# One attention group's division and pair transpose moved out of the run of row maxima, behind the first two maxima of a later group

## What is computed

```python
xn = _layernorm(x)
q = (xn @ wq).reshape(4, 512, 32, 16); k = (xn @ wk).reshape(4, 512, 8, 16); v = (xn @ wv).reshape(4, 512, 8, 16)
# rope on q and k; each of the 8 key heads serves 4 query heads
scores = einsum('bqhd,bkhd->bhqk', q, k) / 4 + causal_mask
attn = softmax(scores)                       # exp(score - row maximum), then a division by the row sum
s = einsum('bhqk,bkhd->bqhd', attn, v).reshape(4, 512, 512) @ wo
g = silu(top-2-of-8 experts: mean of relu(xn @ W_e + b_e))
x = x + s * g
# second layer: layer norm, a long convolution (S4 kernel made from its spectrum), gated by a linear layer
```

## Time and profile before

| | us |
|---|---|
| median of 3 runs | 697.06 (695.39 to 698.77) |
| the profiled execution's own time | 695.48 |
| its span, first to last instruction | 693.3 |
| PE busy | 638.2 (92%) |
| DVE busy | 553.4 (80%) |
| POOL busy | 351.1 (51%) |
| ACT busy | 289.0 (42%) |
| mean granted TensorE clock | 0.97 of full |

### The profile page before, as it was taken

The page is one execution under the profiler, slowest core; times in us unless marked ns, Lnnn a source line. Parts: engine busy times, 40 slices in busy tenths (PEclk is TensorE's granted clock), DMA queues, the critical chain, the costliest instruction groups (busy, mean ns, idle before and its releaser), DMA issues.

```text
span 693.3 us, 12356 instructions
## 1 busy us (share of the span) xinstructions
PE 638.2 (92%) x3560; PEld 344.0 (50%) x3560; DVE 553.4 (80%) x1789; ACT 289.0 (42%) x535; POOL 351.1 (51%) x497
## 2 busy tenths in 40 slices
PE   8999997888989999989999898999998999999997
PEld 4888774433333334333443333443333443488886
DVE  5698898669987777987777798787887887769995
ACT  4353326234443444434454443444344543445441
POOL 3777531636764723466473245646415434566630
PEclk9999999569999999999999999999999999999999
DMA  7599989246667454272653606457063526758851
GB/s 251 151 330 281 331 195 180 50 68 179 106 191 125 98 96 75 40 134 77 114 96 64 92 22 131 106 99 128 20 117 64 142 80 215 152 119 220 201 132 76
DMA packets 55567, 92.67 MB, mean 134 GB/s; under 512 B 10328, under 2 KB 23320, under 8 KB 55504
## 3 DMA queue, kind: packets, MB, share of 16 engines
q1 hardware_dynamic: 41890, 66.45, 41.0%
q0 software_dynamic: 8576, 18.62, 12.7%
q10 hardware_dynamic: 5038, 6.84, 3.9%
HBM read 61.93 MB, written 29.43 MB: 132 GB/s over the span
## 4 chain that ended last, share of the span: by engine, by line
PE 46%; DVE 39%; issue 6%; DMA 3%; POOL 3%; SPq 1%; ACT 1%; ACTq 0%; DVEq 0%; POOLq 0%
DVE bank L1374 19%; PE bank L1644 10%; PE bank L1616 7%; PE bank L1563 6%; PE bank L2072 6%; DVE arena L1374 4%; PE bank L2077 4%; PE bank L991 4%; DMA turned_parts<-qk_parts 3%; DVE arena L1407 2%; PE bank L1655 2%; DVE m_parts L1387 2%; PE bank L1589 2%; PE bank L1600 2%; DVE arena L1424 2%
## 5 line engine op out<-in xcount | busy, mean ns | idle before, releaser
L1374 DVE CUSTOM_DVE_ANT_0 bank<-bank,cst 128x384 f32<-128x384 f32 (+3 forms) x512 | 234.0, 522 | 66.8 <-PE bank L1563 65.2
L1486 ACT ACTIVATE arena<-bank 128x512 f32<-128x512 f32 x320 | 172.7, 600 | 209.6 <-PE bank L1589 149.9
L1321 POOL DMA_INDIRECT arena<-xn_rows,slots_i x156 | 150.1, 962 | 55.0 <-issue 37.3
L1308 POOL TENSOR_SCALAR_AFFINE_SELECT arena<-arena 128x512 f32<-128x512 f32 x128 | 81.0, 647 | 182.9 <-ACT arena L1486 181.8
L1644 PE MATMUL bank<-w_e,arena 128*128 x312 | 160.4, 620 | 0.0
L1563 PE MATMUL bank<-kt,qt 48*128 48x512 f32 (+1 forms) x496 | 119.5, 352 | 15.3 <-DVE arena L1374 12.4
L1563 PEld LDWEIGHTS bank<-kt,qt 48*128 48x128 f32 x496 | 73.6, 193 | 101.6 <-DVE arena L1374 56.3
L1589 PE MATMUL bank<-qt,kt 50*128 50x512 f32 x256 | 92.2, 464 | 0.6 <-ACT arena L1486 0.6
L1616 PE MATMUL bank<-arena 128*32 128x512 f32 (+3 forms) x1024 | 88.0, 455 | 2.7 <-ACT arena L1486 2.3
L1644 PEld LDWEIGHTS bank<-w_e,arena 128*128 128x128 f32 x312 | 53.7, 192 | 57.5 <-issue 54.2
L1374 DVE DVE_READ_ACCUMULATOR2_ANT arena<- 128x1 f32 x512 | 72.0, 141 | 0.0
(11 more groups left out here) (168 smaller groups left out, 954.3 us busy)
## 6 DMA issues: line engine op xcount, KB each, us to landing
qt<-turned_parts SPq DMA_DIRECT2D x96, 128.0 KB
turned_parts<-qk_parts SPq DMA_DIRECT2D x8, 1280.0 KB
expert_rows<-arena SPq DMA_DIRECT2D x39, 256.0 KB
w_e<-in_L_ffn_W_e ACTq DMA_DIRECT2D x24, 256.0 KB, 6.1
kt<-turned_parts SPq DMA_DIRECT2D x96, 64.0 KB, 5.5
arena<-in_L_attn_x SPq DMA_DIRECT2D x16, 256.0 KB, 5.8
xn_rows<-arena SPq DMA_DIRECT2D x16, 256.0 KB, 5.7
w_e<-in_L_attn_x SPq DMA_DIRECT2D x16, 256.0 KB
```

The source lines that it names most:

```text
L1308: g.affine_select(out=diag, in_=diag, compare_op=ALU.is_ge, fill=0.0, base=0, pattern=[[0, 2], [0, HALF], [1, P]], channel_multiplier=-1). ...
L1321: e.indirect_dma_start(xg[m % 2][:, n * P:(n + 1) * P], None, xn_q, bass.IndirectOffsetOnAxis(ap=slots_i[:, n, m:m + 1], axis=0)).then_inc ...
L1374: i = v.tensor_tensor_reduce(out=part, in0=part, in1=const("mask")[:, S - w:], scale=1.0, scalar=LOWEST, op0=ALU.add, op1=ALU.max, accum_o ...
L1486: nc.scalar.activation(pt[:, s, first:second + 1:second - first].rearrange("p c r q -> p c (r q)"), s2_bank(b, h, n).rearrange("p (c x) -> ...
```

## The change

`finish` is split in `rows_of` and `divided` (reciprocal, multiplication, and for an odd group the pair transpose). In an iteration with h > 0 that has a following group, only `rows_of` stays at its place after the maxima of parts 2 to 4; `divided` comes after `maxima_rows` and the maxima of parts 0 and 1. With h = 0, and in the last iteration, the order is as before. Nothing is added or taken away, and no engine but DVE changes its order.

```diff
+            def divided(b, h):
+
                 normalise(b, h)
                 if h % 2:
                     pair_rows(b, h // 2)
+
+            def finish(b, h):
+
+                rows_of(b, h)
+                divided(b, h)
...
                     if following:
                         for n in (2, 3, 4):
                             maxima(e, *following, n)
-                    finish(*next_group(b, h, -1))
+                    done, later = next_group(b, h, -1), h > 0 and following
+                    rows_of(*done)
+                    if not later:
+                        divided(*done)
                     if following:
                         for n in range(5, NJ):
                             maxima(e, *following, n)
...
                     if after:
                         for n in (0, 1):
                             maxima(e, *after, n)
+                    if later:
+                        divided(*done)
```

More of the change, by code:

```diff
@@ L1424, in pair_rows @@
                 v.transpose(ot[:, (b * PAIRS + i) % (PAIRS + 1)].rearrange("p t f -> p (t f)"), o2.rearrange("p q c -> p (q c)")).then_inc(b_o2, 1)
-            def finish(b, h):
-                rows_of(b, h)
+            def divided(b, h):
                 normalise(b, h)
```

## The result

| | before | after |
|---|---|---|
| median of 4 runs | 696.22 us (694.08 to 698.77) | 688.43 us (687.84 to 689.93) |
| ratio of the medians' runs, 95% interval | | 0.9902 [0.9874, 0.993] |
| the profiled execution's own time | 695.48 | 689.93 |
| its span | 693.3 | 687.8 |
| PE busy; DVE busy | 638.2; 553.4 | 634.1; 551.5 |

The ratio is worth 696.22 x 0.0098 = 6.8 us (4.9 to 8.8 us). The kernel is faster, by about half of the 12.5 us forecast. The median lies inside the range, 679.5 to 691.5 us.

A forecast was written before the change was run, and what follows sets the result against it. PE, busy 92%, bounds the kernel; only its idle time that DVE ends can be won. 12.0 (even h) + 2.0 (odd h) - 1.5 (given back) = 12.5 us, from 697.06 to 684.6 us; range 679.5 to 691.5 us.

The forecast's parts named there:

- Even h, waits before pass 1: 12 even-h iterations: PE's waits at L1563 for maxima to free a bank go, part of 14.4 us counted with the turn.
- Even h, the turn: PE's wait at L1600 for last maxima and split goes, less 2.4 us over eight iterations; even h gives 12.0 us.
- the four without selects in the way: Iterations (0, 2), (0, 4), (1, 4), (2, 4): PE's waits of 1.76 us each go, the split being through before the selects.
- The rival of the selects: POOL's selects hold the split in all twelve even-h iterations, 0.7 us each: 6.5 us won, 690.6 us; chance 0.20.
- Odd h: 15 odd-h iterations, where 0.70 us of DVE work moves: 2.0 us won, ends 0 and 6 us.
- everything goes: Rival: all waits except those of h = 0 vanish, as earlier splits also precede odd-h selects: 22 us, 675 us; chance 0.07.
- Given back after (0, 2), (1, 2), (2, 2): Moved work delays the next iteration's first maxima, so PE waits 0.5 us three times: 1.5 us lost, ends 0 and 4.1 us.
- if PE starts to wait for DVE before its expert or value matmuls: One of the signs in the changed profile that would show the prediction wrong.
- The slower rival: Moved work delays expert transposes, so POOL's gathers and selects come late: 16.6 us against 12.5 us, 701 us; chance 0.05.

The follow-up runs named there:

- the second job: Four kernels beside the kernel before (683.67 us): the change again (676.91 us), and three with iteration (3, 6) at its old order, two of them with one further edit.
- The run with the select waiting: Changed kernel with iteration (3, 6) in its old order, plus POOL's third select waiting for the split of the maxima: 668.77 us, ratio 0.9784; measured again, 667.69 us, 0.9768.
- the first pair of traces: Profiles of the kernel before and the changed kernel from the first measurement: 695.48 and 689.93 us.
- (3, 6) put back: Changed kernel, but iteration (3, 6) keeps its division and pair transpose at the old place: 671.46 us, ratio 0.982 of the kernel before.
- the first job: Four kernels beside the kernel before (697.0 us): the change in even h alone, in odd h alone, and both orders without expert gathers of tiles 2 to 38.
- the third job: Four kernels beside the kernel before (683.14 us), among them the unchanged order for its own trace (682.69 us) and the order of before with only the select's wait (672.81 us).

## Why the prediction was partly right

- **Even h, waits before pass 1.** Right: 8.6 us went to nothing, and the 14.4 us of waits counted were 14.5.
- **Even h, the turn.** This is the term that failed: "nearer to nothing since part of the pair will be over by then", 2.4 us left. It was 7.1 us. In the seven iterations like (1, 2) the split is held until the pair of selects ends, so the turn comes 0.29 us behind the pair both before and after. The forecast took the 0.29 us of the earlier trace rows for a split that slips through; it was already a held one. There the split took 0.56 us and PE waited 0.51 to 0.53 us each. The forecast built the turn from rows of two iterations, 3.06 us for PE and 2.84 us for DVE, a slack of 0.22 us; measured in (1, 2) after the change they are 2.80 and 3.32 us. Even h as a whole gave 7.4 us, not 12.0. Of the four without selects in the way, (0, 2), (1, 4) and (2, 4) kept 0.34, 0.42 and 0.46 us and (0, 4) 1.99 us; in the second job, free of late results, they kept 0.32, 0, 0 and 0.14 us.
- **The rival of the selects** was nearer in mechanism. In size, its 690.6 us against 697.06 x 0.9902 = 690.2 us is luck: it had neither the waits before the values nor (3, 6), and their 9.3 us were made up by odd h, by what is given back and by PE's busy time. The split is held in all seven of those iterations, though it takes 0.56 to 0.57 us and not 1.25 us. The run with the select waiting shows it. The rule of the Trainium skill ("SBUF — State Buffer", "Who interferes with whom"), that whichever of VectorE and GpSimd issues first holds the shared ports for its whole instruction, fits: the splits that lie behind the start of a select take up to 1.25 us, and 0.17 us once the select is behind the split. The 1.25 us of (1, 1) span both selects of the pair, of 0.65 us each, which is more than the rule's one instruction. The forecast read the rule as holding the split in all twelve iterations; where the split comes first, as in (1, 4) after, it took 0.17 us.
- **Odd h.** Under-sized: 4.7 us (turn 7.9 to 3.9, pass 1 2.7 to 2.0), not 2.0. (1, 1), (2, 1) and (3, 1) kept their waits, 0.77 us each, as said; but in (1, 3) and (2, 3) it fell from 0.92 and 0.88 to 0.31 and 0.49 us, and in (3, 3) from 1.02 us to nothing, where the split at 521.25 us now starts ahead of the selects at 521.73 us, as the rival "everything goes" had it. That order is not stable: in the second job the same kernel waited 0.78 us there.
- **Given back after (0, 2), (1, 2), (2, 2).** Over-sized: PE's new waits there are 0.2 us each in two places, not 1.5 us in all.
- **Missing, first:** the waits before the values, +7.1 us in the first pair of traces and +3.8 us in the second. The text said it would be wrong "if PE starts to wait for DVE before its expert or value matmuls"; it does, by way of ACT's queue. The slower rival looked at gathers behind transposes; the price came from transposes behind gathers and from late results beside them.
- **Missing, second:** (3, 6). The prediction says that after most iterations the moved work is hidden by DVE's 65.2 us of waits, and named the three where it is not; it never looked at the last one, where S4's longest chain ends at a PE wait of 0.44 us. It cost 2.15 us of wait; whether the slow clock behind it belongs to it stays open.

The idle time of the first pair adds up to 7.4 + 4.7 + 0.4 - 7.1 - 2.15 = 3.3 us against 5.5 us between the spans. Over the whole span PE's idle time fell by only 1.4 us, from 693.3 - 638.2 = 55.1 us to 687.8 - 634.1 = 53.7 us, mostly since the transposes of x in stage a, which the change does not touch, waited 3.7 us instead of 2.3 us. The other 4.1 us are PE's busy time, 638.2 to 634.1 us, and no run shows why it fell. So that the median fell inside the range is in part luck too: what was forecast too well or left out (the turn, the values, (3, 6)) and what was forecast too low a gain (odd h, what is given back) partly cancelled.

## What to carry to other kernels

Moving work behind a burst frees the first waits in it, but the last one is set by the whole chain: measure that chain in the very iteration, end to end, not from pieces of others. For each iteration that is changed, the last ones above all, look at what stands behind the new place, and follow the result through the queues of the engines behind it (here DVE's copy, ACT's DMA, its exponentials, PE's values). And where a short instruction of VectorE is on the path and a long one of GpSimd holds it, try letting GpSimd's wait: that one wait was worth 9.8 us without the change, and the best kernel here, with both and (3, 6) put back, ran in 667.69 us against 683.14 us.

## What the runs showed of the hardware

**Late results beside gathers, in some jobs.** The same kernel before took 697 us in the runs shown first and in the first job, and 683 us in the other two. The 13.2 us between the two spans lie in stage b alone (436.9 and 423.6 us from the first maxima of (0, 1) to the last turn), and there mostly in iterations with many gathers. Iterations (1, 0) to (1, 3), with 12 gathers, took 13.60, 14.77, 13.71 and 14.87 us in one trace and 13.58, 14.77, 13.69 and 14.88 us in the other; (1, 4) to (1, 7), with 28 gathers, took 15.79, 14.52, 14.40 and 14.83 us against 14.68, 14.30, 13.71 and 14.05 us. The number of gathers does not decide it alone: (1, 3) has 7 of the 12 and did not change, while (2, 0) and (3, 0), with one each, took 14.71 and 14.74 us against 13.60 and 13.59 us. Without gathers stage b took 420.0 us in the job of 697 us too. What can be seen late is the news of PE's results. DVE's copy waits for the turn (total, times, longest) in the first traces before and after, then in the third job's before and the second job's change:

```profile
DVE arena L1397 <- PE bank L1600: 7.8, 14, 1.5
```

```profile
DVE arena L1397 <- PE bank L1609: 12.9, 20, 1.2
```

```profile
DVE arena L1397 <- PE bank L1600: 4.3, 11, 0.5
```

```profile
DVE arena L1397 <- PE bank L1609: 4.3, 11, 0.5
```

These 3.5 us are a part of the 13.2 us. Another part is PE's own wait for ACT before the first matmul of an expert tile, 4.4 us in the first trace before. Here it is in the first trace after, then in the second job's change:

```profile
L1651 PE MATMUL bank<-be,sel_e 128*128 128x512 bf16 x39 | 15.6, 400 | 4.6 <-ACT arena L1505 4.6
```

```profile
L1651 PE MATMUL bank<-be,sel_e 128*128 128x512 bf16 x39 | 15.4, 395 | 0.0
```

The rest is not placed. Why some jobs have it and others not stays open; the record gives one chip number for the first and the third job, and only the first has late results. Open is also the path by which a gather delays another engine's semaphore.

**The clock differs between kernels by as much as a wait.** In the second job the six runs of the change had a mean granted clock of 0.967 to 0.972 and those with (3, 6) put back 0.975 to 0.980; the single stretch at 1.2 GHz at L762 is one part of it. With the select's wait in the same job it was 0.966 to 0.972 again, with that stretch back, though the turn's waits had fallen by 7.6 us; the medians, 671.46 and 668.77 us, differ by 2.7 us. What decides whether the stretch falls there, the runs do not show.
